# L1 attention: the softmax weights normalised by ScalarE instead of GpSimd, with a new order of steps

## The reference

```python
v = (x @ wqv_w.T + wqv_b).reshape(b, t, 3 * h, d)
q, vf, vb = (v[:, :, :h], v[:, :, h:2 * h], v[:, :, 2 * h:])
k = x[:, :, None, :] * wk[None, None]
a = _l1_scores(q, k)      # a[b,s,t,h] = -sum_w |q[b,s,h,w] - k[b,t,h,w]| / sqrt(w)
a = jnp.concatenate([a, jnp.zeros((b, 1, t, h), a.dtype)], axis=1)
a = jax.nn.softmax(a, axis=1)[:, :t]
bf = jnp.einsum('bsdh,bshw->bdhw', a, vf)
bb = jnp.einsum('bdsh,bshw->bdhw', a, vb)
o = (bf + bb).sum(axis=2).reshape(b, t, d)
y = o * jax.nn.sigmoid(1.702 * o)
y = y @ fanin_w.T + fanin_b
return x + y
```

## Time and profile before

| | us |
|---|---|
| median of 3 runs (lowest to highest) | 2432.77 (2432.23 to 2436.34) |
| the profiled execution | 2433.18 |
| its span, first to last instruction | 2431.3 |
| busy in the span: PE, DVE, POOL, ACT | 2149.1, 2071.3, 1766.5, 1573.1 |
| busy in the L1 attention's loop, 706 to 2324 us (1618.0): PE, DVE, POOL, ACT | 1520.4, 1498.7, 1545.8, 1278.0 |

### The profile page before, as it was taken

How to read it: one execution, slowest core, us unless ns; L and a number is a source line. 1 busy time by engine, 2 the same in 40 slices (tenths; PEclk the granted TensorE clock), 3 DMA queues, 4 the chain that set the end, 5 groups by cost and what they waited for, 6 DMA issues and landing times.

```text
span 2431.3 us, 48360 instructions
## 1 busy us (share of the span) xinstructions
PE 2149.1 (88%) x13399; PEld 1011.8 (42%) x13399; DVE 2071.3 (85%) x2497; ACT 1573.1 (65%) x4028; POOL 1766.5 (73%) x1033
## 2 busy tenths in 40 slices
PE   5566999999749999999999999999999999999978
PEld 3352333333213444444444444444444444444457
DVE  2877777777879999999999999999999999999974
ACT  1333343343328877877878777787777778777756
POOL 0111333333439999999999999999999999999943
PEclk8787999999869999999999999999999999999979
DMA  4302333233212221222212222122221222212201
GB/s 125 81 1 49 80 76 74 69 78 80 49 30 56 56 56 47 56 52 56 55 49 56 50 56 55 49 56 51 56 55 48 55 52 55 56 47 55 52 20 33
DMA packets 169426, 135.47 MB, mean 56 GB/s; under 512 B 45661, under 2 KB 151070, under 8 KB 169247
## 3 DMA queue, kind: packets, MB, share of 16 engines
q1 hardware_dynamic: 159850, 118.02, 19.6%
q10 hardware_dynamic: 9532, 16.91, 2.9%
HBM read 10.51 MB, written 4.19 MB: 6 GB/s over the span
## 4 chain that ended last, share of the span: by engine, by line
POOL 60%; PE 18%; DVE 11%; issue 5%; ACT 3%; POOLq 1%; ACTq 1%; DMA 1%; DVEq 0%; SPq 0%
POOL absd L1671 57%; PE pp L658 3%; DVE absd L1493 3%; POOL attk L1682 3%; PE pp L683 1%; PE pp L951 1%; PE pp L679 1%; DVE score L1553 1%; ACT absd L1080 1%; PE pp L684 1%; PE pp L680 1%; ACTq L1067 1%; DVE yw L1477 1%; PE pp L582 1%; PE pp L640 1%
## 5 line engine op out<-in xcount | busy, mean ns | idle before, releaser
L1553 DVE TENSOR_REDUCE score<-pp 128x16 f32<-128x1024 f32 x1280 | 1481.3, 1213 | 131.7 <-PE pp L851 131.6
L1671 POOL TENSOR_TENSOR absd<-absd 128x2560 f32<-128x2560 f32 x635 | 1447.1, 2279 | 68.3 <-ACT absd L1147 24.3
L851 PE MATMUL pp<-blocks,pick 128*128 128x512 f16 x2560 | 737.9, 381 | 28.7 <-DVE score L1553 20.7
L1147 ACT ACTIVATE absd<-pp 128x512 f32<-128x512 f32 x1280 | 695.5, 598 | 66.7 <-PE pp L839 54.4
L839 PE MATMUL pp<-blocks,pick 128*128 128x512 f16 x1280 | 416.0, 383 | 42.3 <-ACT absd L1147 26.9
L1638 POOL TENSOR_TENSOR absd<-absd,yw 128x512 f32<-128x512 f32 x112 | 142.2, 1270 | 307.0 <-DVE yw L1477 307.0
L851 PEld LDWEIGHTS pp<-blocks,pick 128*128 128x128 f16 x2560 | 206.7, 97 | 345.8 <-DVE score L1553 235.0
L1080 ACT ACTIVATE absd<-pp 128x512 f32<-128x512 f32 x256 | 149.5, 597 | 203.4 <-PE pp L680 156.7
L1493 DVE SCALAR_TENSOR_TENSOR absd<-pp,absd 128x512 f32<-128x512 f32 x256 | 171.6, 686 | 81.2 <-ACT absd L1080 68.3
L839 PEld LDWEIGHTS pp<-blocks,pick 128*128 128x128 f16 x1280 | 113.7, 97 | 281.1 <-ACT absd L1147 177.7
L1177 ACT ACTIVATE expd<-attn 128x65 f32<-128x65 f32 x512 | 160.8, 328 | 0.0
(11 more groups left out here) (229 smaller groups left out, 2682.3 us busy)
## 6 DMA issues: line engine op xcount, KB each, us to landing
blocks<-qk SPq DMA_DIRECT2D x1032, 64.0 KB, 2.0
blocks<-gT SPq DMA_DIRECT2D x128, 128.0 KB
blocks<-gT ACTq DMA_DIRECT2D x128, 128.0 KB
attn<-score SPq DMA_DIRECT2D x256, 64.0 KB, 2.1
xs<-xn SPq DMA_DIRECT2D x66, 32.0 KB, 1.8
big<-in_wrb_t SPq DMA_DIRECT2D x1, 2064.0 KB
big<-in_x_rows SPq DMA_DIRECT2D x4, 512.0 KB, 6.3
token_rows<-big SPq DMA_DIRECT2D x8, 256.0 KB, 2.0
```

The source lines that it names most:

```text
L851: mm = pe.matmul(ps[bank + n], pick[:, unit % 8 + n, :], blocks[:, b, unit // 16, unit // 8 % 2, :], start=True, stop=True)
L1147: nc.scalar.activation(absd[odd][:, 16 * u + 8 * n:16 * u + 8 * n + 8, :], ps[4 + n].rearrange("p (h w) -> p h w", w=D), ACT.Abs).then_inc ...
L1553: dve.tensor_reduce(score[:, odd, b, 16 * d:16 * d + 16], pp[:, bank:bank + 2, :].rearrange("p n (h w) -> p (n h) w", w=D), AX.X, ALU.add, ...
L1671: nc.gpsimd.tensor_tensor(x[:, :, 0:w], x[:, :, 0:w], x[:, :, w:2 * w], ALU.add).then_inc(X["tree"], 1)
```

## The change

Normalising moves from POOL to ACT: eight ACTIVATEs with the function Copy and the reciprocal as scale per partition, one a head, in two groups of four. In PE, ACT and DVE the steps of a pair stand in a new order. In PE, `values_b` and `values_f` go behind the first two A steps, `turn`, `sum_e`, `queries` and `turn_e` move up, `low` down, the two strings of `ORDERS` change (in the first image the last D step now stands behind the E step), `turn_y` moves up into the pair before and `fan_in` to the head of the pair. In DVE, `finish` stands behind the first reduction, and `reciprocals` at the end of the pair before. SP's refill for the first image waits for its last D step, which is now the last reader.

```diff
@@ -36,7 +36,7 @@
 
 
 
-ORDERS = ("DADADADDADDDADDE", "DDADADDADADDADDE")
+ORDERS = ("DADADDADDADDADED", "DADDADADDADDADDE")
 ND, NP = ORDERS[0].count("D"), ORDERS[0].count("A")
 NA = NP + 1
 W_SCALE = 64.0
@@ -450,7 +450,10 @@
 
                 if not first:
 
-                    sp.wait_ge(X["diffA"], 2 * NA * (2 * (p - 1) + b + 1))
+                    if b == 0:
+                        sp.wait_ge(X["diffD"], ND * (2 * (p - 1) + 1))
+                    else:
+                        sp.wait_ge(X["diffA"], 2 * NA * (2 * (p - 1) + 2))
                 for kind in range(2):
                     for part in range(2):
                         if b == 0:
@@ -856,26 +859,24 @@
             def pair(q, odd, at):
                 def extra(b, k):
                     if b == 0:
-                        if k == 4 and at >= 3:
-                            turn_y(q - 3)
-                        if k == 6 and at >= 3:
-                            fan_in(q - 3)
+                        if k == 1 and at >= 1:
+                            values_b(q - 1, 1 - odd, at)
+                        if k == 3 and at >= 1:
+                            values_f(q - 1, 1 - odd)
+                        if k == 4:
+                            turn(q + 1, at)
                         if k == 7 and at >= 1:
-                            values_f(q - 1, 1 - odd)
-                        if k == 8:
-                            turn(q + 1, at)
-                        if k == 10 and at >= 1:
                             sum_e(q - 1, at == 1)
-                        if k == 12:
+                        if k == 10:
                             queries(q + 1, at)
+                        if k == 13 and at >= 1:
+                            turn_e(q - 1)
                         if k == 15:
                             low(q + 1, 1 - odd, 0)
-                            if at >= 1:
-                                turn_e(q - 1)
                     else:
-                        if k == 0:
+                        if k == 2:
                             keys(q + 1, 1 - odd)
-                        if k == 3:
+                        if k == 5:
                             low(q + 1, 1 - odd, 1)
                         if at >= 2:
                             if k == 7:
@@ -885,9 +886,11 @@
                                 attend(q - 2, odd, 1)
                             if k == 11:
                                 attend(q - 2, odd, 2)
-
-                if at >= 1:
-                    values_b(q - 1, 1 - odd, at)
+                            if k == 14:
+                                turn_y(q - 2)
+
+                if at >= 3:
+                    fan_in(q - 3)
                 for b in range(2):
                     image(q, b, at, extra)
 
@@ -903,7 +906,6 @@
                     pair(2 * i + odd, odd, 4)
             last = PAIRS - 1
             values_b(last, 1, 4)
-            turn_y(last - 2)
             values_f(last, 1)
             fan_in(last - 2)
             pe.wait_ge(X["sum"], last - 1)
@@ -1179,6 +1181,16 @@
                 if part == 3:
                     op.then_inc(X["exp"], 1)
 
+            def normalise(p, part, first):
+                if part == 0:
+                    act.wait_ge(X["zr"], p + 1)
+                    if not first:
+                        act.wait_ge(X["o_ps"], p)
+                for n in range(4 * part, 4 * part + 4):
+                    op = nc.scalar.activation(attk[:, n, :], expd[:, n, 0:S], ACT.Copy, scale=zst[:, 1, n:n + 1])
+                if part:
+                    op.then_inc(X["attk"], 1)
+
             def turned_attn(p):
                 act.wait_ge(X["attq_ps"], p + 1)
                 nc.scalar.copy(attq[:].rearrange("p a b -> p (a b)"), ps[6]).then_inc(X["attq"], 1)
@@ -1194,46 +1206,47 @@
 
             def pair(q, odd, at):
                 s, first = 2 * q, at == 0
+                absolute(s, 0, 0, q, first)
                 if at >= 1:
                     values_b(q - 1, 1 - odd, at < 3)
-                absolute(s, 0, 0, q, first)
                 absolute(s, 0, 1, q, first)
-                if at >= 3:
-                    turned_y(q - 3)
+                prepare_x(q + 1, 1 - odd)
+                if at >= 2:
+                    normalise(q - 2, 0, at == 2)
                 absolute(s, 0, 2, q, first)
                 if at >= 1:
                     values_f(q - 1, 1 - odd)
-                prepare_x(q + 1, 1 - odd)
+                    copy_e(q - 1)
                 absolute(s, 0, 3, q, first)
-                if at >= 1:
-                    copy_e(q - 1)
+                if at >= 2:
+                    normalise(q - 2, 1, at == 2)
                 absolute(s, 0, 4, q, first)
-                high_q(q + 1, False)
-                low(q + 1, 0)
-                absolute(s, 0, 5, q, first)
                 if at >= 1:
                     take_e(q - 1, 1 - odd, at - 1)
-                high_k(q + 1)
+                high_q(q + 1, False)
+                absolute(s, 0, 5, q, first)
+                low(q + 1, 0)
                 s += 1
                 absolute(s, 1, 0, q, first)
+                high_k(q + 1)
                 absolute(s, 1, 1, q, first)
                 low(q + 1, 1)
                 absolute(s, 1, 2, q, first)
-                if at >= 1:
-                    exponentials(q - 1, 0, at == 1)
                 if at >= 2:
                     turned_attn(q - 2)
+                if at >= 1:
+                    for part in range(2):
+                        exponentials(q - 1, part, at == 1)
                 absolute(s, 1, 3, q, first)
                 if at >= 1:
-                    exponentials(q - 1, 1, at == 1)
+                    for part in range(2, 4):
+                        exponentials(q - 1, part, at == 1)
                 if at >= 2:
                     gate_o(q - 2)
                 absolute(s, 1, 4, q, first)
-                if at >= 1:
-                    exponentials(q - 1, 2, at == 1)
+                if at >= 2:
+                    turned_y(q - 2)
                 absolute(s, 1, 5, q, first)
-                if at >= 1:
-                    exponentials(q - 1, 3, at == 1)
 
             act.wait_ge(pads, PADS)
             prepare_x(0, 0)
@@ -1248,7 +1261,6 @@
                     pair(2 * i + odd, odd, 4)
             last = PAIRS - 1
             values_b(last, 1, False)
-            turned_y(last - 2)
             values_f(last, 1)
             copy_e(last)
             take_e(last, 1, 4)
@@ -1273,11 +1285,15 @@
                     nc.scalar.activation(hm[:, l + 1, g % 2, P * j:P * j + P], ps[2 + l][:, P * j:P * j + P], ACT.Relu,
                                          bias=wsel[g % 3][:, l, j, HID:HID + 1]).then_inc(M[f"h{l + 1}"], 1)
 
+            normalise(last - 1, 0, False)
+            normalise(last - 1, 1, False)
             turned_attn(last - 1)
             gate_o(last - 1)
             turned_y(last - 1)
             for part in range(4):
                 exponentials(last, part, False)
+            normalise(last, 0, False)
+            normalise(last, 1, False)
             root(0)
             turned_attn(last)
             for i in range(G4 + 3):
@@ -1561,13 +1577,12 @@
                         dve.wait_ge(X[f"spread{b}"], SPREAD * (q - 1))
                     for d in range(ND):
                         reduce(2 * q + b, odd, b, d)
-                        if b == 0 and d == 3:
-                            if at >= 3:
-                                finish(q - 3, slot)
-                            if at >= 2:
-                                reciprocals(q - 2)
+                        if b == 0 and d == 0 and at >= 3:
+                            finish(q - 3, slot)
                         if b == 1 and d == 7 and at >= 2:
                             gated(q - 2)
+                        if b == 1 and d == 9 and at >= 1:
+                            reciprocals(q - 1)
 
             dve.wait_ge(X["hx"], 1)
             for q in range(4):
@@ -1576,7 +1591,6 @@
                 for odd in range(2):
                     pair(2 * i + odd, odd, bass.ds(2 * i + odd - 3, 1), 4)
             last = PAIRS - 1
-            reciprocals(last - 1)
             finish(last - 2, slice(last - 2, last - 1))
 
             dve.wait_ge(X["pooled"], 2 * last + 1)
@@ -1675,18 +1689,9 @@
                 nc.gpsimd.tensor_tensor(score[:, odd, b, 16 * ND:16 * ND + 16 * NP].unsqueeze(2), x[:, :, 0:1], x[:, :, 1:2],
                                         ALU.add).then_inc(X["pooled"], 1)
 
-            def normalise(p, first):
-                pool.wait_ge(X["zr"], p + 1)
-                if not first:
-                    pool.wait_ge(X["o_ps"], p)
-                nc.gpsimd.tensor_tensor(attk[:], expd[:, :, 0:S], zst[:, 1, :].unsqueeze(2).to_broadcast([P, HEADS, S]),
-                                        ALU.mult).then_inc(X["attk"], 1)
-
             def pair(q, odd, at):
                 if at >= 1:
```

(5 more changed lines are left out.)

## The result

The change made the kernel faster by 1.5%: the median is 2395.49 us (four runs, 2395.03 to 2395.77) against 2432.50 before (four runs, 2429.2 to 2436.34); the ratio is 0.9847, with a 95% interval of 0.983 to 0.9864. The forecast was 2398. The profiled execution took 2395.6 us, its span is 2393.8. In the new file lines stand 3 to 16 further down: the D step is L854, A L842, E L846, `values_b` L753, `values_f` L760, `attend` L786 and L791, the reduction L1569, `gated` L1559, `reciprocals` L1554, `finish` L1564, ACT's `absolute` L1149 and L1152, `turned_attn` L1196, POOL's tree L1685 and L1689. New is `normalise`, L1190.

What follows compares the result with a forecast made beforehand. POOL's loop of 25.36 us a pair was taken as the bound, PE with DVE close behind at 25.22. At 24.66 a pair, 60 x (25.32 - 24.66) = 40, less 5 for the tail, is 35: 2433.2 - 35 = 2398, range 2379 to 2423.

Steps and rivals of the forecast that it cites:

- The walk: New pair's PE and DVE steps timed slot by slot: idle 1.31 on 23.15 of DVE work, 24.46 us a pair.
- the sore spot: Before the first image's third reduction: values_b and values_f in neighbouring gaps leave DVE idle 0.85 us.
- surcharge: 0.2 us a pair added to 24.46, since the same pricing of the old order gave 25.01 against 25.22 traced.
- D7': Eighth D step of the second image, at attend; starts 0.43 + 0.10 + 1.24 after the one before, DVE idle 0.18.
- D6': Seventh D step of the second image, from whose start the next one's distance at attend is counted.
- the old 0.66 at `attend`: DVE idle in the old order, laid to PE waiting 0.38 for ACT's turned-weights copy behind two exponentials; forecast 0.24 or 0.2.
- A head: One 128x64 ACT activation, priced at 0.21 us; eight make 1.7 a pair, with room for 1.05 more.
- rival 2: ACT's queue becomes the loop if a head costs 0.50: 25.93 a pair, 2480 us; chance 0.10.
- The tail: Last two pairs normalised on ACT without cover: + 1.7 and + 3.4, together + 5 us.
- The first: Rival: POOL stays the bound, idle of 0.85 comes out smaller, 24.36 a pair, 2380 us; chance 0.15.
- The third: Rival: a head on ACT costs 0.35, 0.1 more a pair and 2 in the tail, 2406 us; chance 0.08.
- The fourth: Rival: two projections with the copy wait between cost 0.5 more, about 25.2 a pair, no gain, 2431 us; chance 0.08.

Runs made afterwards that it cites:

- experiment 3: Changed kernel with PE's values_f one D step later, turn behind the next, and ACT's queue reordered to match: 2379.56 us, ratio 0.9787.
- 10: Changed kernel with values_f one D step later and the last two pairs normalised by POOL: 2373.05 us, ratio 0.9751.
- experiment 9: Kernel before, old order, normalisation on ACT in its idle gaps, reciprocals behind the next pair's first reduction: 2435.28 us, ratio 1.0007.
- experiment 1: Changed kernel's new order, with normalisation left on POOL in loop and tail: 2432.38 us, ratio 0.9997.
- Experiment 11: Changed kernel with ACT's copy of the turned weights put back behind two heads of exponentials: 2393.55 us, ratio 0.9833.
- experiment 12: Changed kernel with the turned weights' copy behind two heads of exponentials and the second image's old string of steps: 2440.47 us, ratio 1.0033.
- 6: Changed kernel with four more heads a pair on ACT, written to a spare tile, also in the tail: 2404.47 us, ratio 0.988.
- experiment 7: Changed kernel with eight more heads a pair on ACT, written to a spare tile, also in the tail: 2459.47 us, ratio 1.0106.
- experiment 4: Changed kernel with the last two pairs normalised by POOL, the loop untouched: 2390.6 us, ratio 0.983.

## Why the prediction was right, and where it was not

*The bound, and the two loops.* Right. POOL was the bound, its floor without L1682 is near 24.36 (experiments 3 and 10: 24.38 and 24.34), and PE with DVE alone take 25.2 in the old order (experiment 9: 25.24). That taking work from POOL alone would gain next to nothing was shown by 9, that the order alone gains nothing by 1.

*The walk.* Right in place and size: the sore spot is before the third reduction, where the walk put 1.99 from start to start and the trace has 1.98; the ninth reduction of the second image 1.585 for 1.58. Experiment 3 showed that the sore spot is the two projections in neighbouring gaps: with one moved by a step, PE and DVE go below POOL.

*The sum of the walk: a slip and a surcharge.* D7' starts 0.43 + 0.10 + 1.24 = 1.77 behind D6'. By the prediction's own rule a D step may come 1.135 + 0.36 behind the one before until DVE idles; that leaves 1.77 - 1.135 - 0.36 = 0.28 of idle, and not the 0.18 that was written. The trace has 1.41 - 1.135 = 0.28. The 0.20 in the bracket looks like the written number only because brackets count differently. With this put right the idle is 1.41 and the walk gives 24.56, for 24.58 measured. On top stood 0.2, because the same walk of the old order fell short by that. In the new order only 0.02 of it shows. Another 0.10 made good the slip, and the rest, 60 x 0.08 = 4.8 us, is gain that the forecast left out. That 0.2 is the term of the sum that was mis-sized; that it and the slip pulled in opposite directions is luck. The old walk's steps are not on record, so whether it held the same slip (0.13 of its shortfall is at `attend`) stays open.

*The cause of the old 0.66 at `attend`: half shown.* The prediction laid PE's wait to the copy standing behind two exponentials, and credited the new place in ACT's queue. Experiment 11 put it back behind them and lost nothing. So that place is not needed: the new string, with a D step between the A step and the turning, is enough to remove the wait, and 12 brought it back by the string alone. In experiment 12's rows the two exponentials hold the copy up from 1506.70 to 1507.31, 0.6 us for a wait of 0.38; so the copy's new place alone, in the old string, might have done it too. That was not run. The walk had counted the slots, so its number did not hang on which of the two did it.

*A head: mis-sized, without consequence.* 0.24 by starts, not 0.21. The 0.21 was the distance from an exponential to the reading of its accumulator, not to another ACTIVATE. The cost is 8 x 0.03 = 0.24 us a pair of ACT, under a room that experiments 6 and 7 measured as 8 x 0.239 + 0.88 to 0.96 = 2.8 to 2.9 us; the prediction had 1.7 + 1.05 = 2.7. It also named the place where that room ends, the A copies ahead of the E step. Beyond it nearly each us is a us: four more heads, from 12 to 16, cost 0.87 for 0.96 of ACT. So rival 2's mechanism, ACT's queue as the loop, is real, and only its price was not: with 16 x 0.24 = 3.8 us of heads, near its 8 x 0.50 = 4.0, experiment 7 is slower than before.

The Trainium skill (ScalarE: Activation LUTs, Rules for kernel authors) budgets about 0.3 us for an ACTIVATE and 0.83 ns an element; for 64 elements that makes an estimate of 0.35 us. The rows agree with it as a length, 344 ns, and not as a price: in a queue of them one takes 0.24. By 0.35 the eight would take 2.8 us a pair, the whole of the measured room. Another section of that page of the Trainium skill (ScalarE: Activation LUTs, What ACT_TABLE_LOAD costs) is nearer: 280 ns and 0.833 ns an element for an ACTIVATE with one operand per partition, less 93 ns by which such instructions in a row overlap, which makes an estimate of 240 ns for 64 elements. The trace agrees, with 239.

*The tail.* +5 forecast, 5.3 in the traces, and experiment 4, which changes only who normalises there, takes 4.7 less. The parts are 2.02 us for eight heads ahead of the turning (forecast 1.7) and, at the table load, 2299.26 - 2281.02 = 18.2 us behind the last reduction. There it stood 2338.78 - 2323.86 = 14.9 before, so 3.3 later, for 3.4 forecast. For the last pair the sign named came too: ACT waits 1.19 for the reciprocal, then does eight heads, then loads the table. PE's wait for the turning of the last but one pair is there, but the trace calls its cause "issue", not ACT.

*The sum.* 44.96 - 5.34 - 2.12 = 37.5 against the forecast 40 - 5 = 35. Two differences partly cancel, which is luck too: the loop gained 5 more, and 2.1 were lost ahead of the attention, where nothing was edited. With one trace of each kernel it is not shown whether that start varies from execution to execution or from kernel to kernel; it lies inside the 6.7 us over which it varies in this study.

*The rivals.* The first, POOL still the bound at 2380, needed a smaller sore spot, which the change does not have (1.98 from start to start, as walked); experiment 3 made it smaller and ran in 2379.56. The third, 2406 at 0.35 a head, fell with 0.24. The fourth, no gain through a late copy of `values_b`: the weight loads of `values_f` wait for it in each pair (0.42 us, of which PE's work on the steps before covers nearly all), but PE itself stands idle only 0.09 there.

## What to carry to other kernels

When the busiest engine's loop is only 0.6% longer than the next one (25.36 and 25.22 here), relieving it is worth at most those 0.6%; write both loops down before pricing an edit, and change the order of the second and the load of the first together, since each alone may measure as nothing, as here. Walk the new order slot by slot with distances between starts, compare with distances between starts and not with the brackets, and note the neighbouring gaps that are both filled: here the walk found the spot whose repair gave another 16 us. Work given to an engine with slack can be free in the loop, up to the room there (eight heads of the twelve or so that ACT could take), and is paid in the tail, where nothing covers it; in this kernel it was better left on POOL there.

## What was unexpected of the hardware

A small ACTIVATE occupies ScalarE for less than its length: 0.239 us from start to start at a length of 0.344, for 128x64 from SBUF with a scale per partition. From the exponential of 128x65 to the reading of its accumulator it is 0.21. Whether the copy is dearer by its scale, an operand per partition, or only because another instruction follows, no run here shows.

The table load in the tail costs its 1.28 us and no more: it runs from 2299.26, and in the same timeline the square root behind it starts at 2300.55.

The windows have another thing. In the 6 us behind the attention's last reduction the granted clock was 0.72 before, on its way from the upper to the lower level (2.4 to 1.2 GHz), as this row of the kernel before shows, while after the change it was 1.00 over 6.5 us.

```profile
2323.90:2329.90 6.00, 4.38 (x30) 2.42 (x30) 3.98 (x3) 1.85 (x7) 2.55 (x6) 0.72 0.08 22
```

In both, PE had been at work without long pauses until that reduction and did only some thirty matmuls in the stretch. Why the fall came later after the change stays open; it is part of the 5.3 us only with a sign that favours the change. Its share is small: in experiment 1, with the old division of work in the tail, the clock was still 1.00 over the 12.2 us from 2327.0 on, and behind the last reduction it took 106.4, only 1.0 less than before.
